# Transposes inside the first half of each tile's products, low halves ahead of the gate logits, and an opening in another order

## The chip, the cores and the metric

One core of a Trainium2 chip runs the whole program. The time is device microseconds of one launch, from the first to the last instruction and what lies around it. The kernel before took 1167.78 us (median of three runs, 1166.98 to 1170.35).

## What is computed

The reference is one macaron layer on `x` of 4 sequences x 512 rows x 512 columns: half a step of a feed-forward block with gated low-rank corrections, latent attention with 32 heads, and the feed-forward block again with the same weights.

```python
x = x + 0.5 * ffn(layernorm(x))
x = x + attn(layernorm(x))        # 32 heads, causal, latent keys of 64, rotary parts of 64
x = x + 0.5 * ffn(layernorm(x))

def ffn(x):
    y = x @ W_base.T + b_base
    z = einsum('bth,erh->bter', x, lora_A[active])          # 4 experts, rank 8
    logits = (x @ router_W.T + router_b)[..., active]
    alpha = softmax(log(domain_prior[active] + EPS) + logits)
    return y + einsum('bteo,bte->bto', einsum('bter,eor->bteo', z, lora_B[active]) * 2.0, alpha)
```

## The kernel before, in words

Every engine has its own program, written out by hand, and runs it strictly in the written order; semaphores are the only ties between them. There is no scheduler: the order of the work is the order of the Python statements, and an instruction that waits holds all that stands behind it on its engine.

The work of a sequence `b` is a row of tiles of 128 rows, and an attention over all its heads. A **feed-forward tile** goes through these steps. ScalarE (in the opening VectorE) normalises the rows, `xn` (`norm`, L1163 and L1275). TensorE transposes them in four pieces into the bank `X[0]` (`transpose_x`, L650). ScalarE rounds the transposed rows to `xT_hi` (`xT_high`, L1037), VectorE takes the rest, `xT_lo` (`xT_low`, L1281). TensorE forms three products (high by high, high by low, low by high) for each of 4 blocks of columns (`ffn_products`, L675), in two halves: half 0 is 12 matmuls of 292 columns (256 outputs, 32 of `z`, 4 gate logits), half 1 is 12 of 256. From the end of half 0, VectorE reads the logits and their maximum (`gate_logits`, L1288 and L1290), ScalarE the exponentials (`gate_exponentials`, L1046), VectorE divides and scales `z` by the gates to `za` (`gate_rows`, L1295, L1297, L1306). TensorE transposes `za` (`transpose_z`, L691), ScalarE and VectorE split it into `zT_hi` (L1042) and `zT_lo` (L1314), and TensorE adds the low-rank correction (`lora`, L700). VectorE adds the tile to the rows (`update_rows`, L1321).

A **down tile** makes the latent queries, keys and values of 128 rows: the same normalising and transposing, then `down_products` (L684), two halves of 6 matmuls of 320 columns, `key_rotary` on VectorE (L1331 to L1334), `down_copies` on ScalarE (L1053 to L1055), `transpose_down` on TensorE (L710), and `ckT_high` and `ckT_low`.

These tiles come in three kinds of stage:

- the **opening** (sequence 0, before its attention): weights are transposed and split first (`transpose_base`, `base_high`, `base_low`, `transpose_lora`, `fill_up` L1358), the statistics of the first rows come in between, `gate_row` is spread to all partitions by a matmul (L800), then 4 feed-forward tiles, which I call F0 to F3 here too, then weight folding and 4 down tiles (these alone keep their order);
- the **mixed stage**, between two attentions, three times (near 319, 592 and 865 us): 12 tiles in the order of the table `ORDER`: the next sequence's first feed-forward tiles F0 to F3, then D0, L0, D1, L1, D2, D3, L2, L3, where D are the next sequence's down tiles and L this sequence's last feed-forward tiles;
- the **last stage** (sequence 3): L0 to L3.

On TensorE, tile i stands as: half 0; the transposes of `za` of tile i-1; the transposes of the rows of tile i+1; if tile i-1 is a down tile, its `transpose_down`; half 1; the correction of tile i-1. On VectorE, tile i stands as: `update_rows` of tile i-2 with its statistics; `gate_logits` of i; `z_low` of i-1; `xT_low` of i+1; `ckT_low`; `gate_rows` of i. On ScalarE: `norm` of i+1, `z_high` of i-1, `xT_high` of i+1, `ckT_high`, `gate_exponentials` of i, `down_copies`.

GpSimd makes the inverse deviations of the rows of down tiles (`down_deviations`, L508 to L531); in the opening it also splits the rotary weights in products of several us (L585, L589). ScalarE's queue has three loads of activation tables in the opening, before L1067, before the logarithm of the prior (L1115) and before a first exponential (L1117).

Of the kernel before, what the change touches and what calls it, by code (L numbers as in the profile page):

```python
# [34 lines left out]
P = 128  # L35
NB, S, D = 4, 512, 512
ST = S // P
KC = D // P
# [69 lines left out]
def build(nc, hidden, w_q_down, w_q_up_nope, w_q_up_rope, w_kv_down, w_k_rope, w_uk, w_uv, w_out,  # L108
          W_base, b_base, lora_A, lora_B, router_W, router_b, domain_prior, active,
          rope_cos, rope_sin, rope_cosT, rope_sinT, out):  # L110
    with ExitStack() as ctx:
# [292 lines left out]
        with nc.Block() as block:  # L404
# [240 lines left out]
            def _(pe):  # L645
# [24 lines left out]
                def ffn_products(b, s, half):  # L670

                    a, z = ((0, W0), (W0, WB))[half]
                    for c in range(KC):
                        for j, (xt, w) in enumerate(((xT_hi, wb_hi), (xT_hi, wb_lo), (xT_lo, wb_hi))):
# [5 lines left out]
                def down_products(b, s, half):  # L680

                    for c in (2 * half, 2 * half + 1):
                        for j, (xt, w) in enumerate(((xT_hi, wd_hi), (xT_hi, wd_lo), (xT_lo, wd_hi))):
# [97 lines left out]

                def opening_queries():
# [11 lines left out]
                def opening():  # L794
# [3 lines left out]
                    pe.wait_ge(turns_one, 1)  # L798
                    pe.wait_ge(gate_in, 16 * 2 * NE)
                    nc.tensor.matmul(gate_ps, cosT[0:1, 0:P], gate_row[:], start=True, stop=True).then_inc(gate_spread, 1)  # L800
                    pe.wait_ge(lora_lo_set, 1)
                    for s in range(FIRST, DOWN):
# [4 lines left out]
                        ffn_products(-1, s, 0)  # L807
                        if s > FIRST:
                            if s == FIRST + 1:
                                pe.wait_ge(up_lo, 1)  # L810
                            transpose_z(-1, s - 1)
                        if s + 1 < DOWN:
                            transpose_x(-1, s + 1)
# [54 lines left out]
                def steps(b, order):  # L868

                    for i, s in enumerate(order):  # L870
                        products = ffn_products if s < DOWN else down_products
                        wait_for_products(b, s)
                        products(b, s, 0)
                        if i and order[i - 1] < DOWN:
                            transpose_z(b, order[i - 1])
                        if i + 1 < len(order):
                            transpose_x(b, order[i + 1])
# [156 lines left out]
            def _(act):  # L1034
# [62 lines left out]
                def opening():  # L1097
# [4 lines left out]
                    for c in range(KC):  # L1102
# [4 lines left out]
                                  .rearrange("q (h d) -> q h d", d=DN)).then_inc(nope_in[0], 16)  # L1107
                    xT_high(-1, FIRST)
# [7 lines left out]
                    act.wait_ge(consts_set, 1)  # L1116
                    nc.scalar.activation(warm_slot[:, 0:1], three_halves[0:1, :], ACT.Exp)  # L1117
# [126 lines left out]
            def _(dve):  # L1244
# [160 lines left out]
                def opening():  # L1405
# [4 lines left out]
                    nc.vector.bn_stats(stats[:, 0, :], x_sb[:, 0, :]).then_inc(stats_set, 1)  # L1410
# [29 lines left out]
                    for s in range(FIRST, DOWN):  # L1440
# [7 lines left out]
                        if s + 1 < DOWN:  # L1448
                            xT_low(-1, s + 1)
# [46 lines left out]
                def mixed_steps(b):  # L1496
                    for i, s in enumerate(ORDER):
# [7 lines left out]
                        if s < DOWN:  # L1505
                            gate_logits(b, s)
# [164 lines left out]
```

## Time and profile before

| | |
|---|---|
| runs | 1170.35, 1166.98, 1167.78 us |
| the profiled execution | 1167.57 us, of which 1165.8 us are the span |
| mean granted TensorE clock | 0.992 of full speed |
| busy share: PE, PEld, DVE, ACT, POOL | 95%, 78%, 78%, 54%, 63% |
| chain that ended last | PE 79%, DVE 7%, POOL 7%, ACT 3% |

PE is TensorE's matmuls, PEld its weight loads, DVE VectorE, ACT ScalarE, POOL GpSimd, SP the engine that issues most transfers. A row of the timeline has the start in us from the span's start, the duration, the engine, the line, the operation, the output and the inputs, and in brackets how long the engine had been idle before and what ended that. A matmul's duration covers its whole way through the array; the distance of starts tells how densely they follow each other.

### The profile page before, as it was taken

The numbers are of one execution on the slowest core, as the hardware profiler recorded it, in microseconds if no ns is written. First come the engines' busy times: TensorE is split into PE (matmuls) and PEld (weight loads), VectorE is DVE, ScalarE is ACT, GpSimd is POOL, SyncE is SP. The second block draws the span as 40 slices with busy tenths as digits, with TensorE's granted clock in tenths as the row PEclk, the third lists the DMA queues.
The fourth block names the chain that finished last, engine by engine and source line by source line (L and its number), as shares of the span: only waits on it lengthen the run. The fifth ranks groups of instructions, "written<-read, shape, count | busy, mean of one in ns | idle before, by whom it ended". The sixth has DMA issues, their size and how long they took to land.

```text
span 1165.8 us, 21866 instructions
## 1 busy us (share of the span) xinstructions
PE 1105.7 (95%) x7284; PEld 906.6 (78%) x7284; DVE 908.2 (78%) x2667; ACT 623.9 (54%) x1733; POOL 740.0 (63%) x951
## 2 busy tenths in 40 slices
PE   5896999999998999999999899999999899999997
PEld 4755788888797788888788678888888678888876
DVE  4767888888676888878776888788867787888855
ACT  3554655555454655555535555655545466555542
POOL 2406977887432978787631887787723598877841
PEclk9998999999999999999999999999999999999998
DMA  9660000000101000000101000000010100000000
GB/s 286 179 194 1 1 1 1 1 1 1 37 10 64 2 1 2 1 1 1 37 1 37 37 2 1 2 1 2 1 37 28 47 1 1 1 1 2 1 1 37
DMA packets 22248, 30.96 MB, mean 27 GB/s; under 512 B 9302, under 2 KB 11094, under 8 KB 21498
## 3 DMA queue, kind: packets, MB, share of 16 engines
q1 hardware_dynamic: 19770, 24.85, 6.7%
q10 hardware_dynamic: 2368, 4.72, 1.2%
q8 instruction: 59, 0.97, 0.3%
q14 instruction: 51, 0.42, 0.1%
HBM read 22.23 MB, written 4.19 MB: 23 GB/s over the span
## 4 chain that ended last, share of the span: by engine, by line
PE 79%; DVE 7%; POOL 7%; ACT 3%; issue 2%; SPq 1%; DMA 1%; POOLq 0%; DVEq 0%
PE Y L983 15%; PE Y L957 12%; PE XZ L942 11%; PE Y L906 10%; PE XZ L922 6%; PE XZ L923 6%; PE XZ L921 5%; PE Y L675 4%; POOL prob L631 3%; PE XZ L675 2%; POOL qT_lo L542 2%; PE XZ L650 2%; POOL q_sums L537 2%; DVE xT_lo L1281 1%; ACT xT_hi L1037 1%
## 5 line engine op out<-in xcount | busy, mean ns | idle before, releaser
L1228 ACT ACTIVATE prob<-XZ,small 128x512 f32<-128x512 f32 (+3 forms) x512 | 266.3, 525 | 282.8 <-DVE small L1622 282.8
L631 POOL TENSOR_TENSOR prob<-prob,small 128x512 f32<-128x512 f32 (+3 forms) x512 | 360.7, 721 | 50.1 <-DVE small L1576 40.4
L1622 DVE CUSTOM_DVE_ANT_0 XZ<-XZ,mask 128x512 f32<-128x512 f32 (+3 forms) x512 | 247.9, 506 | 114.6 <-PE XZ L923 110.5
L537 POOL TENSOR_TENSOR q_sums<-q_sums,q_turned 64x512 f32<-64x512 f32 (+2 forms) x130 | 164.2, 1263 | 201.5 <-DVE q_turned L1564 200.1
L942 PE MATMUL XZ<-ident,prob 128*128 128x128 f32 x1280 | 196.3, 276 | 3.2 <-POOL prob L631 2.9
L921 PE MATMUL XZ<-kT_hi,qT_hi 128*128 128x512 f32 (+3 forms) x512 | 176.9, 345 | 12.7 <-ACT prob L1228 6.8
L542 POOL TENSOR_TENSOR qT_lo<-q_sums,qT_hi 128x512 fp32r<-128x512 f32 (+2 forms) x130 | 165.2, 1271 | 31.9 <-ACT qT_hi L1195 31.8
L942 PEld LDWEIGHTS XZ<-ident,prob 128*128 128x128 f32 x1280 | 149.5, 140 | 43.2 <-POOL prob L631 10.6
L922 PE MATMUL XZ<-kT_lo,qT_hi 128*128 128x512 f32 (+3 forms) x512 | 165.4, 323 | 0.0
L923 PE MATMUL XZ<-kT_hi,qT_lo 128*128 128x512 f32 (+3 forms) x512 | 165.2, 323 | 0.0
L957 PE MATMUL Y<-probT,ckv 128*64 128x384 f32 (+2 forms) x1280 | 152.3, 384 | 0.0
L390 ACT ACTIVATE probT<-XZ 128x512 f32<-128x512 f32 x192 | 114.9, 598 | 66.0 <-PE XZ L942 64.8
L957 PEld LDWEIGHTS Y<-probT,ckv 128*64 128x64 f32 x1280 | 81.8, 136 | 60.7 <-issue 47.3
L921 PEld LDWEIGHTS XZ<-kT_hi,qT_hi 128*128 128x128 f32 x512 | 97.2, 190 | 22.8 <-issue 7.7
L983 PE MATMUL Y<-wo_hi,oT_hi 128*128 128x512 f32 x256 | 110.9, 433 | 1.5 <-DVE x_sb L1580 1.4
L1580 DVE TENSOR_TENSOR x_sb<-Y,x_sb 128x512 f32<-128x512 f32 x128 | 87.8, 686 | 29.4 <-PE Y L983 29.1
L1228 ACT ACTIVATION_READ_ACCUMULATOR prob<-XZ,small 128x1 f32 x512 | 101.9, 199 | 0.0
L923 PEld LDWEIGHTS XZ<-kT_hi,qT_lo 128*128 128x128 f32 x512 | 97.3, 190 | 5.5
L922 PEld LDWEIGHTS XZ<-kT_lo,qT_hi 128*128 128x128 f32 x512 | 97.7, 191 | 4.8
L983 PE MATMUL Y<-wo_hi,oT_lo 128*128 128x512 f32 x256 | 101.1, 395 | 0.0
L983 PE MATMUL Y<-wo_lo,oT_hi 128*128 128x512 f32 x256 | 100.2, 391 | 0.0
L1195 ACT ACTIVATE qT_hi<-q_sums 128x512 fp32r<-128x512 f32 (+2 forms) x130 | 80.2, 617 | 19.0 <-POOL q_sums L537 19.0
(220 smaller groups left out, 2162.0 us busy)
## 6 DMA issues: line engine op xcount, KB each, us to landing
wout_nat<-in_L_attn_w_out_dram SPq DMA_DIRECT2D x16, 512.0 KB, 5.0
out_dram<-x_sb SPq DMA_DIRECT2D x16, 256.0 KB, 2.0
x_next<-_attn_hidden_states_dram SPq DMA_DIRECT2D x12, 256.0 KB, 3.4
x_sb<-x_next SPq DMA_DIRECT2D x12, 256.0 KB, 2.3
wbase_nat<-in_L_ffn_W_base_dram ACTq DMA_DIRECT2D x1, 1024.0 KB, 5.7
x_sb<-_attn_hidden_states_dram ACTq DMA_DIRECT2D x4, 256.0 KB, 7.0
nope_a<-_L_attn_w_q_up_nope_dram ACTq DMA_DIRECT2D x1, 1024.0 KB, 5.4
rope_a<-_L_attn_w_q_up_rope_dram SPq DMA_DIRECT2D x1, 1024.0 KB, 8.0
```

What stands on the lines that cost most here:

```text
L537: nc.gpsimd.tensor_tensor(q, q, turned, ALU.add).then_inc(q_sum_set, 1)
L542: nc.gpsimd.tensor_tensor(qT_lo[par][:, head, cols], q_sums[par][:, head, cols], f32(qT_hi[par][:, head, cols]), ALU.subtract).then_inc(qT ...
L631: last = nc.gpsimd.tensor_tensor(prob[u % RING][:, c:c + w], prob[u % RING][:, c:c + w], inv_sum[:, u % RING, m:m + 1].broadcast_to([P, w] ...
L906: last = nc.tensor.matmul(bank[:, cols], w, c, start=(j == 0), stop=(j == 4))
L921: nc.tensor.matmul(bank[:, c:c + w], high, kT_hi[:, 0:w], start=True, stop=False)
L922: nc.tensor.matmul(bank[:, c:c + w], high, kT_lo[:, 0:w], start=False, stop=False)
L923: last = nc.tensor.matmul(bank[:, c:c + w], low, kT_hi[:, 0:w], start=False, stop=True)
L942: last = nc.tensor.transpose(probT_ps[v % 2][:, at], prob[v % RING][:, at], ident[:])
L957: last = nc.tensor.matmul(o_ps[64 * h:64 * h + 64, column * P:(column + n) * P], ckv[:, j, :], probT[:, HEAD_BLOCKS * h + at:HEAD_BLOCKS * ...
L983: last = nc.tensor.matmul(bank, o[buffer][:, rows], w, start=(k == 0 and j == 0), stop=(k == 1 and j == 2))
L1228: last = nc.scalar.activation(prob[u % RING][:, c:c + w], score_ps[u % 2][:, c:c + w], ACT.Exp, bias=neg_max[:, u % RING, m:m + 1], scale= ...
L1622: last = nc.vector.tensor_tensor_reduce(bank, bank, mask[:, S - w:S], -1.0, HIGHEST, ALU.add, ALU.min, neg_max[:, u % RING, m:m + 1])
```

## The change

The calls stay the same, and so do all operands; one activation is added on ScalarE (a first logarithm). Their order changes in five ways.

1. In `ffn_products` and `down_products` the transposes (`za` of the tile before, rows of the next) are called in the middle of half 0: after 6 of its 12 matmuls, in a down tile after 3 of its 6. `transpose_down` stays behind half 0.
2. On VectorE `z_low` and `xT_low` stand ahead of `gate_logits`.
3. In the opening the spreading of `gate_row` moves from ahead of F0's products into their middle.
4. In the opening VectorE takes the first rows' moments ahead of two weight splits, their deviations, normalising and `fill_up` ahead of the other rows' statistics.
5. ScalarE loads the logarithm's table ahead of the first `xT_high`.

```diff
-                def ffn_products(b, s, half):
+                def ffn_products(b, s, half, inside=None):
                     a, z = ((0, W0), (W0, WB))[half]
                     for c in range(KC):
+                        if c == KC // 2 and inside:
+                            inside()
                         for j, (xt, w) in enumerate(((xT_hi, wb_hi), (xT_hi, wb_lo), (xT_lo, wb_hi))):
...
-                def down_products(b, s, half):
+                def down_products(b, s, half, inside=None):
                     for c in (2 * half, 2 * half + 1):
+                        if c == 1 and inside:
+                            inside()
...
+                def spread_gates():
+                    pe.wait_ge(turns_one, 1)
+                    pe.wait_ge(gate_in, 16 * 2 * NE)
+                    nc.tensor.matmul(gate_ps, cosT[0:1, 0:P], gate_row[:], start=True, stop=True).then_inc(gate_spread, 1)
...
                     transpose_lora()
-                    pe.wait_ge(turns_one, 1)
-                    pe.wait_ge(gate_in, 16 * 2 * NE)
-                    nc.tensor.matmul(gate_ps, cosT[0:1, 0:P], gate_row[:], start=True, stop=True).then_inc(gate_spread, 1)
                     pe.wait_ge(lora_lo_set, 1)
...
-                        ffn_products(-1, s, 0)
-                        if s > FIRST:
-                            if s == FIRST + 1:
-                                pe.wait_ge(up_lo, 1)
-                            transpose_z(-1, s - 1)
-                        if s + 1 < DOWN:
-                            transpose_x(-1, s + 1)
+
+                        def transposes(s=s):
+                            if s == FIRST:
+                                spread_gates()
+                            else:
+                                if s == FIRST + 1:
+                                    pe.wait_ge(up_lo, 1)
+                                transpose_z(-1, s - 1)
+                            if s + 1 < DOWN:
+                                transpose_x(-1, s + 1)
+
+                        ffn_products(-1, s, 0, transposes)
                         ffn_products(-1, s, 1)
...
-                        products(b, s, 0)
-                        if i and order[i - 1] < DOWN:
-                            transpose_z(b, order[i - 1])
-                        if i + 1 < len(order):
-                            transpose_x(b, order[i + 1])
+
+                        def transposes(i=i):
+                            if i and order[i - 1] < DOWN:
+                                transpose_z(b, order[i - 1])
+                            if i + 1 < len(order):
+                                transpose_x(b, order[i + 1])
+
+                        products(b, s, 0, transposes)
                         if i and order[i - 1] >= DOWN:
                             transpose_down(b, order[i - 1])
...
+                    act.wait_ge(consts_set, 1)
+                    nc.scalar.activation(warm_slot[:, 0:1], three_halves[0:1, :], ACT.Ln)
                     xT_high(-1, FIRST)
...
                     nc.scalar.activation(prior_row, prior_raw[:], ACT.Ln).then_inc(prior_ln, 1)
-                    act.wait_ge(consts_set, 1)
-                    nc.scalar.activation(warm_slot[:, 0:1], three_halves[0:1, :], ACT.Exp)
+                    nc.scalar.activation(warm_slot[:, 1:2], three_halves[0:1, :], ACT.Exp)
...
                     nc.vector.bn_stats(stats[:, 0, :], x_sb[:, 0, :]).then_inc(stats_set, 1)
+                    dve.wait_ge(stats_set, 1)
+                    row_moments(FIRST).then_inc(var_set, 1)
                     base_low(2)
                     base_low(3)
-                    dve.wait_ge(stats_set, 1)
-                    row_moments(FIRST).then_inc(var_set, 1)
+                    deviations(0, FIRST, 1, 1)
+                    norm(FIRST)
+                    fill_up()
                     for t in range(1, ST):
                         dve.wait_ge(x_in[t], 16)
                         nc.vector.bn_stats(stats[:, t, :], x_sb[:, t, :]).then_inc(stats_set, 1)
-                    deviations(0, FIRST, 1, 1)
-                    norm(FIRST)
                     dve.wait_ge(stats_set, ST)
...
-                    fill_up()
                     xT_low(-1, FIRST)
...
+                        if i and ORDER[i - 1] < DOWN:
+                            z_low(b, ORDER[i - 1])
+                        if i + 1 < MIXED:
+                            xT_low(b, ORDER[i + 1])
                         if s < DOWN:
                             gate_logits(b, s)
-                        if i and ORDER[i - 1] < DOWN:
-                            z_low(b, ORDER[i - 1])
                         if i == 3:
                             deviations(4 + 2 * b, 0, ST, GROUPS_0 + GROUPS * b + 3)
-                        if i + 1 < MIXED:
-                            xT_low(b, ORDER[i + 1])
```

The opening's loop and `last_steps` move `gate_logits` behind `z_low` and `xT_low` in the same way.

TensorE, mixed stage, tile L0 (the tile after D0): `xn_79` are the rows of D1, `down_91` those of D0, `xT_*_82` and `xT_*_84` L0's transposed rows. Before:

```order
L675 MATMUL Y<-wb_hi,xT_lo_84 128x292
L675 MATMUL Y<-wb_hi,xT_hi_82 128x292
L675 MATMUL Y<-wb_lo,xT_hi_82 128x292
L675 MATMUL Y<-wb_hi,xT_lo_84 128x292
L675 MATMUL Y<-wb_hi,xT_hi_82 128x292
L675 MATMUL Y<-wb_lo,xT_hi_82 128x292
L675 MATMUL Y<-wb_hi,xT_lo_84 128x292
L650 MATMUL XZ<-ident,xn_79 128x128 x4
L710 MATMUL Y<-ident,down_91 128x128 x3
L675 MATMUL Y<-wb_hi,xT_hi_82 128x256
```

And now:

```order
L677 MATMUL Y<-wb_hi,xT_lo_84 128x292
L650 MATMUL XZ<-ident,xn_79 128x128 x4
L677 MATMUL Y<-wb_hi,xT_hi_82 128x292
L677 MATMUL Y<-wb_lo,xT_hi_82 128x292
L677 MATMUL Y<-wb_hi,xT_lo_84 128x292
L677 MATMUL Y<-wb_hi,xT_hi_82 128x292
L677 MATMUL Y<-wb_lo,xT_hi_82 128x292
L677 MATMUL Y<-wb_hi,xT_lo_84 128x292
L714 MATMUL Y<-ident,down_91 128x128 x3
L677 MATMUL Y<-wb_hi,xT_hi_82 128x256
```

The next rows' transposes have moved ahead of six products; the down tile's transposes have not moved.

VectorE, mixed stage, tile F3 (`zT_lo_89` is of F2, `xT_lo_83` of D0, the five `newton` to `shift` rows are the deviations of L0 to L3). Before:

```order
L1288 TENSOR_TENSOR small<-XZ,small 128x4
L1290 TENSOR_REDUCE small<-small 128x1
L1314 TENSOR_TENSOR zT_lo_89<-XZ,zT_hi_87 64x128
L1260 TENSOR_TENSOR newton<-rough 128x4
L1262 TENSOR_TENSOR newton<-newton,var_eps 128x4
L1264 TENSOR_SCALAR newton<-newton 128x4
L1266 TENSOR_TENSOR rstd<-newton,rough 128x4
L1269 SCALAR_TENSOR_TENSOR shift<-moments,rstd 128x4
L1281 TENSOR_TENSOR xT_lo_83<-XZ,xT_hi_81 128x512
L1295 RECIPROCAL small<-small 128x1
L1297 TENSOR_SCALAR small<-small 128x4
L1306 TENSOR_TENSOR za_86<-XZ,small 128x32 x2
```

And now:

```order
L1329 TENSOR_TENSOR zT_lo_89<-XZ,zT_hi_87 64x128
L1296 TENSOR_TENSOR xT_lo_83<-XZ,xT_hi_81 128x512
L1303 TENSOR_TENSOR small<-XZ,small 128x4
L1305 TENSOR_REDUCE small<-small 128x1
L1275 TENSOR_TENSOR newton<-rough 128x4
L1277 TENSOR_TENSOR newton<-newton,var_eps 128x4
L1279 TENSOR_SCALAR newton<-newton 128x4
L1281 TENSOR_TENSOR rstd<-newton,rough 128x4
L1284 SCALAR_TENSOR_TENSOR shift<-moments,rstd 128x4
L1310 RECIPROCAL small<-small 128x1
L1312 TENSOR_SCALAR small<-small 128x4
L1321 TENSOR_TENSOR za_86<-XZ,small 128x32 x2
```

The logits and their maximum (L1288 and L1290, now L1303 and L1305) stand behind `xT_lo`, and the reciprocal, which needs ScalarE's exponentials, follows them with no `xT_lo` in between.

ScalarE, opening, from the first rows' high half to the second's (`xT_hi_81` is F0's, `xT_hi_82` F1's). Before:

```order
L1037 ACTIVATE xT_hi_81<-XZ 128x512
L1110 ACTIVATE wb_hi<-Y 128x4x36
L1113 ACTIVATE lora_up<-XZ 128x512
L1115 ACT_TABLE_LOAD
L1115 ACTIVATE small<-prior_raw 128x4
L1117 ACT_TABLE_LOAD
L1117 ACTIVATE small<-small 1x1
L1037 ACTIVATE xT_hi_82<-XZ 128x512
```

And now:

```order
L1123 ACT_TABLE_LOAD
L1123 ACTIVATE small<-small 1x1
L1051 ACTIVATE xT_hi_81<-XZ 128x512
L1126 ACTIVATE wb_hi<-Y 128x4x36
L1129 ACTIVATE lora_up<-XZ 128x512
L1131 ACTIVATE small<-prior_raw 128x4
L1132 ACT_TABLE_LOAD
L1132 ACTIVATE small<-small 1x1
L1051 ACTIVATE xT_hi_82<-XZ 128x512
```

The logarithm's load has moved to the front; the exponential's load still stands between the prior and F1's high half.

## Rows read from the trace of the kernel before

**Rows 1.** Page, part 1: busy time and share of the span, by engine.

```profile
PE 1105.7 (95%) x7284; PEld 906.6 (78%) x7284; DVE 908.2 (78%) x2667; ACT 623.9 (54%) x1733; POOL 740.0 (63%) x951
```

**Rows 2.** Waits, first mixed stage (317 to 374 us): total us, times, longest.

```profile
PEld Y L675 <- issue: 1.4, 4, 0.5
...
PEld XZ L684 <- issue: 0.5, 1, 0.5
...
PEld Y L684 <- issue: 0.3, 1, 0.3
```

**Rows 3.** Timeline, first mixed stage, tiles F1 and F2: start us, us, engine, line.

```profile
324.62 0.60 PE L650 MATMUL XZ<-ident,xn 128*128 128x128 f32 x4
...
325.75 0.29 ACT L1046 ACTIVATE small<-small 128x4 f32<-128x4 f32 x1
...
325.89 0.69 DVE L1281 TENSOR_TENSOR xT_lo<-XZ,xT_hi 128x512 fp32r<-128x512 f32 x1 [0.47 <-ACT xT_hi L1037]
...
326.03 0.80 ACT L1163 ACTIVATE xn<-x_next,shift,rstd 128x512 f32<-128x512 f32 x1
...
326.50 0.15 DVE L1295 RECIPROCAL small<-small 128x1 f32<-128x1 f32 x1
...
326.95 0.29 DVE L1306 TENSOR_TENSOR za<-Y,small 128x32 f32<-128x32 f32 x2
...
329.88 0.13 DVE L1288 TENSOR_TENSOR small<-Y,small 128x4 f32<-128x4 f32 x1
...
330.24 0.30 ACT L1046 ACTIVATE small<-small 128x4 f32<-128x4 f32 x1 [0.34 <-DVE small L1290]
```

**Rows 4.** Timeline, first mixed stage, tile F3 and the rows of D0.

```profile
329.79 0.18 DVE L1253 BATCH_NORM_AGGREGATE moments<-stats 128x2 f32<-128x6 f32 x1
...
332.55 0.81 ACT L1163 ACTIVATE xn<-x_next,shift,rstd 128x512 f32<-128x512 f32 x1 [1.92 <-POOL shift L531]
...
333.41 0.66 PE L650 MATMUL XZ<-ident,xn 128*128 128x128 f32 x4 [0.31 <-ACT xn L1163]
```

**Rows 5.** Timeline, first mixed stage, tile L0 behind D0, and L0's gates in D1.

```profile
338.90 0.37 PE L675 MATMUL Y<-wb_hi,xT_hi 128*128 128x292 f32 x1
...
339.53 0.83 ACT L1163 ACTIVATE xn<-x_next,shift,rstd 128x512 f32<-128x512 f32 x1
...
340.58 0.60 PE L650 MATMUL XZ<-ident,xn 128*128 128x128 f32 x4
...
343.56 0.29 DVE L1306 TENSOR_TENSOR za<-Y,small 128x32 f32<-128x32 f32 x2
343.91 0.33 PE L691 MATMUL XZ<-ident,za 128*128 128x128 f32 x1
```

**Rows 6.** Timeline, first mixed stage, tile L2 and the first queries behind it.

```profile
359.47 0.66 PE L650 MATMUL XZ<-ident,xn 128*128 128x128 f32 x4 [0.24 <-ACT xn L1163]
...
362.21 0.47 PE L906 MATMUL XZ<-cq_hi,wq_hi 128*128 128x512 f32 x1 [0.34 <-DVE kT_lo L1343]
```

**Rows 7.** Timeline, opening: fill-up, gate spread, table load, F2's exponentials, F3's gates.

```profile
15.89 0.20 DVE L1358 COPY up_nat<-up_b 128x128 f32<-128x128 f32 x1
...
19.52 0.56 PE L800 MATMUL Y<-gate_row,cosT 1*128 1x8 f32 x2 [0.98 <-DMA gate_row<-_L_ffn_domain_prior_dram]
...
20.92 1.28 ACT L1117 ACT_TABLE_LOAD   x1
...
33.90 0.29 ACT L1046 ACTIVATE small<-small 128x4 f32<-128x4 f32 x1
...
39.05 1.72 DVE L1297 TENSOR_SCALAR small<-small 128x4 f32<-128x4 f32 x1
```

**Rows 8.** Timeline, last stage: first product of L0, transposes of L1's rows.

```profile
1142.83 0.58 PE L675 MATMUL XZ<-wb_hi,xT_hi 128*128 128x292 f32 x1 [1.83 <-DVE xT_lo L1281]
...
1145.99 0.72 PEld L650 LDWEIGHTS XZ<-ident,xn 128*128 128x128 f32 x4 [0.26 <-ACT xn L1163]
```

**Rows 9.** Windows, last stage: busy us and counts by engine, granted TensorE clock, DMA share, GB/s.

```profile
1143.00:1148.00 5.00, 5.00 (x22) 4.74 (x23) 1.36 (x8) 1.67 (x5) 1.03 (x2) 0.50 0.01 3
```

More of the change, by code:

```diff
@@ L1444, in opening @@
                             norm(s + 1)
-                        gate_logits(-1, s)
                         if s > FIRST:
@@ L1449, in opening @@
                             xT_low(-1, s + 1)
+                        gate_logits(-1, s)
                         gate_rows(-1, s)
@@ L1544, in last_steps @@
                             update_rows(b, s - 2)
-                        gate_logits(b, s)
                         if s:
@@ L1549, in last_steps @@
                             xT_low(b, s + 1)
+                        gate_logits(b, s)
                         gate_rows(b, s)
```

## The prediction

> **What bounds the kernel now.** I read the engines' shares first, then the waits of one mixed stage, then its timeline tile by tile, then the two ends of the program. TensorE is busy 95% of the span [rows 1], so only its gaps can be won, and any new one counts in full. In the first mixed stage the waits before a tile's first product, which is what low halves ahead of the logits can remove, are 1.4, 0.5 and 0.3 us, 2.2 together [rows 2]. Three such stages give 6.6, the most that edit can bring there. The reader should then look at who feeds the transposes, since the change asks for their inputs sooner and puts six products behind them.
>
> **Two loops, in the old timeline.** From the rows' transposes (324.62) it is 1.27 us to the start of `xT_low` (325.89), which holds VectorE 0.61 (to 326.50); from the logits (329.88) it is 0.36 to the exponentials (330.24); from the exponentials (325.75) 0.28 to the next `norm` (326.03) and 1.20 to `za` (326.95) [rows 3]. From `norm` (332.55) it is 0.86 to the transposes of what it wrote (333.41) [rows 4], and from `za` (343.56) 0.35 to its transposes (343.91) [rows 5]. Twelve products take 1.68 (338.90 to 340.58) [rows 5], so six take 0.84; three down products I take as 0.46, an estimate from 0.84 by columns and count (3 x 320 against 6 x 292).
>
> **The mixed stage with the change.** Moving the transposes makes them wanted 0.84 us sooner in a feed-forward tile. Moving the logits makes the exponentials later: the old ones stood 1.13 behind the rows' transposes (324.62 to 325.75) [rows 3]; the new ones stand 1.27 + 0.61 + 0.36 = 2.24 behind them. From one pair of transposes, the rows after next can then be transposed 2.24 + 0.28 + 0.86 = 3.38 later, and the gates 2.24 + 1.20 + 0.35 = 3.79 later. What TensorE does between: 0.35 for the transposes, 0.87 for the other six products (0.84 and a change of weights), half 1 of 1.47 (0.84 x 2 by 256 to 292 columns), a correction of about 0.47 (an estimate, the length of a 512-column product [rows 6]), and the next six products 0.84: 4.0 in all. Between two feed-forward tiles the loops close (3.38 and 3.79 against 4.0). Around a down tile they don't. Tile by tile, the start of the next tile against its old place (an estimate, good to 0.3 each):
>
> - F0 -0.3: a wait of rows 2 goes. F1 +0.35: no correction stands in F0, so the gates are wanted at 4.0 - 0.47 = 3.53, and come at 3.79; the rest is rounding. F2 +0.1, inside the error.
> - F3 +1.1: D0's rows go through GpSimd; their transposes waited before the change already, 0.31 [rows 4], so all of the 0.84 is lost. The moments that GpSimd starts from (329.79, 2.76 ahead of `norm` [rows 4]) now stand behind VectorE's low half, about 0.5 later (0.61, less what VectorE idled). A removed wait gives 0.3 back.
> - D0 +0.2: F3's gates are wanted behind three down products, 0.35 + 0.87 + 1.47 + 0.47 + 0.46 = 3.6, and come at 3.79.
> - L0 +0.65: `norm` of D1's rows starts at 339.53 and allows 339.53 + 0.86 = 340.39, transposes at 340.58 [rows 5]: a slack of 0.19 against a demand 0.84 sooner. Queued behind the wait: L0's other products and all else of TensorE.
> - D1 -0.05 (gates +0.2, a removed wait -0.3); L1 +0.25 (as L0, plus a removed wait); D2 -0.1; D3 -0.3.
> - L2 +0.8: L3's rows were late before, by 0.24 [rows 6], so the demand 0.84 sooner is lost whole, and six products now stand between these transposes and `transpose_down`, whose copies the first queries waited for (362.21) [rows 6].
>
> The sum is +2.7 a stage, 8.1 for three. The lower bound keeps only waits shown by rows where the slack was gone (L0 0.65, L2 0.84, F3 0.84, together 2.3) and takes off half of the 2.2: +1.2. The upper one leaves the removed waits standing: +3.7. Nothing else hides this: the products put behind the waits were the cover.
>
> **The last stage.** TensorE starts L0 at 1142.83 with idle time before, at a granted clock of 0.50 (the 1.2 GHz level) in 1143 to 1148 [rows 8, 9]: 22 matmuls in 5.00 us. L1's rows are ready only for 1145.99, where TensorE already waited 0.26 [rows 8]. Now six products end at about 1144.4 (1142.83 + 6 x 5.00/22 and the first's start), TensorE idles 1.5, and six products of about 0.23 each, 1.4, come after. L0's later products run faster than that where the clock has risen, and the wait before the next tile's first product goes: I take +0.8, bounds +0.4 and +1.5.
>
> **The opening.** The spread of `gate_row` started at 19.52 behind its DMA [rows 7], so it can't be sooner; behind six products that start when `xT_low` and the split LoRA weights are there it comes between 19.5 and 20.8. `fill_up` stood at 15.89 and did not wait [rows 7]; sooner it may wait for its transfer. From the spread on, the gates, a table load of 1.28 (20.92) and the same two loops lead to the exponentials of F2, at 33.90 before, 14.38 behind the spread [rows 7]. In the new order the low half no longer stands behind logits that wait for the prior; by the loops I get 14.0. F2's exponentials matter since ScalarE's weight copies stand behind them and those feed GpSimd's products, beside which F3's gate division took 1.72 (39.05) [rows 7], not the 0.2 of others. So the opening moves by -0.2, bounds -0.4 (the spread at 19.52) and +0.9 (at 20.8).
>
> **Parts at nothing.** The added logarithm is one column of one row on ScalarE ahead of the first `xT_high`, where ScalarE waits for TensorE; its table load only moves. Without that cover it costs one load, 1.28 [rows 7].
>
> **The sum.** The profiled execution is 1167.57 us, 0.2 under the median of the three runs. 1167.57 + 8.1 + 0.8 - 0.2 = 1176.3. The bounds together give 1167.57 + 3.6 + 0.4 - 0.4 = 1171.2 and 1167.57 + 11.1 + 1.5 + 0.9 = 1181.1.
>
> **The rivals.**
> 1. *Faster: the inputs are in time.* If the rows of the tile after a feed-forward one behind a down tile are ready 0.84 sooner too, only the removed waits remain: -6.6, and -1.0 if the opening's first products start a microsecond sooner, 1160.0. The point that decides is the slack at L0: it must exceed 0.84, and rows 5 show 0.19. For it: between feed-forward tiles the loops close, and `norm` at L0 had no idle time ahead of it [rows 5], so some other order of ScalarE's work could bring it sooner. Against it: three places waited before already [rows 4, 6, 8]. 0.10.
> 2. *Even: stalls and removed waits cancel.* If VectorE's lag doesn't reach the exponentials, only L0, L1 and L2 stall, 0.65 + 0.65 + 0.84 = 2.1 a stage, against 2.2 removed: 1167.57 + 0 + 0.8 = 1168.4, within 1167 to 1171. For it: VectorE was idle 0.3 to 0.5 in each of these tiles [rows 3]. 0.16.
> 3. *The clock.* In the last stage the granted clock was 0.50 while TensorE came out of idle time [rows 9]. If the new gap of 1.5 puts the rise off by as much, the twelve products of half 1 that ran partly at the high level cost up to 12 x 0.23 / 2 = 1.4 more: 1177.7. 0.13.
> 4. *One table load for both functions.* The load at 20.92 follows a logarithm and precedes an exponential [rows 7]. If the logarithm moved ahead made the exponential's load unnecessary, the gates would come up to 1.28 sooner: 1175.0. The order of the changed kernel keeps a load there, and the trace has it after a logarithm. 0.02. The Trainium skill (page "ScalarE: Activation LUTs", section "Table sets: the hidden batching unit") says that one set has both functions, so that a logarithm and then an exponential need one load of about 2.7 us; the trace disagrees on both, with a load between them, of 1.28 us.
>
> **Chances and range.** My forecast, slower by 3.6 to 13.5 us, has 0.59; rivals 3 and 4 are slower too, 0.15: slower by over 0.3% together 0.74 (0.3%, 3.5 us, is about what a measurement of this kernel can tell from no change). Rival 2 has 0.16, and gives "within 0.3%"; rival 1, 0.10, is faster. The range leaves out rival 1 and the lower part of rival 2: 1169 to 1182, the upper end that of the bounds and of the clock. The likeliest cases' own range is 1171.2 to 1181.1.
>
> **What would show it.** Right: in the mixed stages TensorE waits before the transposes of rows (on ScalarE's `norm`) and of gates (on VectorE's `za`), 0.5 to 1.7 us at F3, L0 and L2; the waits before a tile's first product are gone; the first queries stand about 2.7 later from the stage's start; the last stage has a gap of 1.5 behind its sixth product; F2's exponentials in the opening are within 0.5 of 33.90. Wrong: no waits at these transposes behind down tiles (rival 1); or waits, but the exponentials as early behind the rows' transposes as before (rival 2); or a load missing ahead of the first exponential (rival 4).

## The result, and the profile after

The changed kernel took 1176.57 us (median of four runs, 1175.3 to 1177.3) against 1168.07 (four runs of before): the ratio is 1.0069, with a 95% interval of 1.0051 to 1.0087. It is slower by 8.5 us; 1176.3 was predicted. The total is right. The terms it was summed from are not: the two largest were wrong in opposite directions. A table by stage, in us, from starts of TensorE's rows in the two profiled executions (spans 1165.8 and 1174.6; "last row" is the last pair of L700 or L704):

| | before | after | difference | predicted |
|---|---|---|---|---|
| first product of the first mixed stage | 319.12 | 318.53 | -0.6 | -0.2 |
| from there to the last stage's first product | 823.71 | 830.07 | +6.4 | +8.1 |
| from there to TensorE's last row | 19.33 | 21.84 | +2.5 | +0.8 |
| from there to the end of the span | 3.6 | 4.1 | +0.5 | 0 |
| a mixed stage, F0's first product to the first queries | 43.09 | 45.15 | +2.06 | +2.7 |

The busy time of TensorE hardly moved: the page of the changed kernel has 1107.3 us against [rows 1]. What was added is waiting.

```profile
PE 1107.3 (94%) x7284; PEld 906.6 (77%) x7284; DVE 909.0 (77%) x2667; ACT 627.8 (53%) x1734; POOL 740.1 (63%) x951
```

The waits of the changed kernel's first mixed stage (us in total, times, longest), beside [rows 2]. These are waits of PEld, the weight loads:

```profile
PEld XZ L650 <- ACT xn L1178: 4.9, 5, 1.4
PEld XZ L695 <- DVE za L1321: 2.0, 5, 0.6
...
PEld XZ L920 <- issue: 0.2, 1, 0.2
PEld XZ L688 <- issue: 0.2, 1, 0.2
```

The waits before a tile's first product went from 2.2 us to the 0.2 of L688, as the edit promises. In their place stand 4.9 us for normalised rows and 2.0 for scaled gates. Before, these two were 1.7 and 0.4 in the same stage:

```profile
PEld XZ L650 <- ACT xn L1163: 1.7, 3, 0.7
...
PEld XZ L691 <- DVE za L1306: 0.4, 1, 0.4
```

TensorE's timeline says where the rows were late: at F3, L0, L1, D3 and L2. The brackets of these matmul rows are shorter than the waits of the weight loads at the same places (0.95, 0.70, 0.74, 1.13 and 1.42), since a bracket starts at the end of the matmul before, some 0.3 us behind its start.

```profile
332.68 0.66 PE L650 MATMUL XZ<-ident,xn 128*128 128x128 f32 x4 [0.76 <-ACT xn L1178]
...
340.53 0.66 PE L650 MATMUL XZ<-ident,xn 128*128 128x128 f32 x4 [0.47 <-ACT xn L1178]
...
348.30 0.66 PE L650 MATMUL XZ<-ident,xn 128*128 128x128 f32 x4 [0.51 <-ACT xn L1178]
...
356.06 0.66 PE L650 MATMUL XZ<-ident,xn 128*128 128x128 f32 x4 [0.87 <-ACT xn L1178]
...
360.45 0.66 PE L650 MATMUL XZ<-ident,xn 128*128 128x128 f32 x4 [1.18 <-ACT xn L1178]
```

And ScalarE's timeline around L0's wait says what made the rows late. The normalising at L1178 stands behind the three copies of D0 (L1067 to L1069), and the first of them waits 1.14 us for the key rotary on VectorE. The rows end at 340.48, and TensorE's transposes of them start at 340.53. (At F3 it is another engine: there `norm` waited 1.13 us for GpSimd's deviations, L531.)

```profile
339.17 0.33 ACT L1067 ACTIVATE down<-Y 128x192 f32<-128x192 f32 x1 [1.14 <-DVE k_sin L1347]
339.40 0.27 ACT L1068 ACTIVATE down<-Y 128x128 f32<-128x128 f32 x1
339.55 0.23 ACT L1069 ACTIVATE ckv<-Y 128x64 f32<-128x64 f32 x1
339.66 0.82 ACT L1178 ACTIVATE xn<-x_next,shift,rstd 128x512 f32<-128x512 f32 x1
```

In the last stage the gap behind L0's sixth product is there, 1.37 us, and the granted clock stays at half long after it: the products behind the gap start 0.24 to 0.25 us apart. TensorE's timeline (the last row is the first product after the clock's rise), then the windows (busy us and counts of PE, PEld, DVE, ACT, POOL; granted clock; DMA share; GB/s), to be read against [rows 8, 9]:

```profile
1148.60 0.58 PE L677 MATMUL XZ<-wb_hi,xT_hi 128*128 128x292 f32 x1 [1.82 <-DVE xT_lo L1296]
...
1151.77 1.11 PE L650 MATMUL XZ<-ident,xn 128*128 128x128 f32 x4 [1.37 <-ACT xn L1178]
...
1152.92 0.45 PE L677 MATMUL XZ<-wb_lo,xT_hi 128*128 128x292 f32 x1
1153.17 0.45 PE L677 MATMUL XZ<-wb_hi,xT_lo 128*128 128x292 f32 x1
...
1157.87 0.30 PE L677 MATMUL Y<-wb_hi,xT_lo 128*128 128x292 f32 x1
```

```profile
1149.00:1154.00 5.00, 3.63 (x16) 3.28 (x16) 1.27 (x6) 1.41 (x2) 0.86 (x1) 0.50 0.00 0
1154.00:1159.00 5.00, 5.00 (x29) 5.00 (x28) 1.52 (x8) 1.63 (x5) 0.00 (x0) 0.62 0.00 0
```

The opening's rows answer to [rows 7]: the first product starts 1.85 us sooner (18.16 against 20.01), the gate spread 0.66 later, F2's exponentials at 33.44 against 33.90.

```profile
18.16 0.61 PE L677 MATMUL Y<-wb_hi,xT_hi 128*128 128x292 f32 x1 [1.48 <-DVE wb_lo L1442]
...
20.18 0.56 PE L789 MATMUL Y<-gate_row,cosT 1*128 1x8 f32 x2 [0.19 <-DMA gate_row<-_L_ffn_domain_prior_dram]
```

```profile
21.20 1.28 ACT L1132 ACT_TABLE_LOAD   x1
...
33.44 0.30 ACT L1060 ACTIVATE small<-small 128x4 f32<-128x4 f32 x1 [1.02 <-DVE small L1305]
```

### The profile page after: what moved, and what is told of

The parts are those of the page before. It is cut to its first block, busy times and chain, and to the rows that moved or that the text cites. A ratio compares the mean times of both kernels' runs of the same rounds, so it can differ in the third digit from the quotient of the medians.

```text
span 1174.6 us, 21867 instructions
## 1 busy us (share of the span) xinstructions
PE 1107.3 (94%) x7284; PEld 906.6 (77%) x7284; DVE 909.0 (77%) x2667; ACT 627.8 (53%) x1734; POOL 740.1 (63%) x951
## 4 chain that ended last, share of the span: by engine, by line
PE 77%; DVE 8%; POOL 7%; ACT 4%; issue 2%; SPq 1%; DMA 1%; POOLq 0%; DVEq 0%
PE Y L997 15%; PE Y L971 12%; PE XZ L956 11%; PE Y L920 10%; PE XZ L936 6%; PE XZ L937 6%; PE XZ L935 5%; PE Y L677 3%; POOL prob L631 3%; POOL qT_lo L542 2%; PE XZ L650 2%; POOL q_sums L537 2%; PE XZ L677 2%; ACT xn L1178 1%; DVE xT_lo L1296 1%
## 5 line engine op out<-in xcount | busy, mean ns | idle before, releaser
L631 POOL TENSOR_TENSOR prob<-prob,small 128x512 f32<-128x512 f32 (+3 forms) x512 | 360.6, 721 | 50.2 <-DVE small L1591 40.4
```

The source lines that it names most:

```text
L631: last = nc.gpsimd.tensor_tensor(prob[u % RING][:, c:c + w], prob[u % RING][:, c:c + w], inv_sum[:, u % RING, m:m + 1].broadcast_to([P, w] ...
```

## The experiments

Two questions were open: which edit costs what in the mixed stage, and why the last stage lost three times its term. Each kernel is read first by its stage lengths, since these repeat (the three mixed stages of an execution agree within 0.06 us), and only then by its time. The lengths are all from the profiled execution, the column of attention from the first of the three; the time is the median of the kernel's runs (c1's profiled execution took 1162.39):

| kernel | time, us | first mixed stage starts | mixed stage | first queries to the next mixed stage | last stage |
|---|---|---|---|---|---|
| before | 1168.07 | 319.12 | 43.09 | 229.80 | 19.33 |
| changed | 1176.57 | 318.53 | 45.15 | 229.86 | 21.84 |
| a1 mixed stage as before | 1170.32 | 320.54 | 43.10 | 229.77 | 21.61 |
| a2 normalising ahead | 1168.97 | 318.69 | 41.22 | 232.00 | 21.10 |
| a3 last stage, behind half 0 | 1177.44 | 320.16 | 45.11 | 229.75 | 19.74 |
| a4 last stage, gap filled | 1179.08 | 321.70 | 45.15 | 230.84 | 19.71 |
| b1 inside, old VectorE order | 1177.64 | 320.01 | 45.19 | 229.81 | 21.85 |
| b2 behind, new VectorE order | 1181.4 | 321.78 | 45.55 | 229.79 | 21.12 |
| b3 before, normalising ahead | 1164.48 | 319.34 | 42.01 | 230.82 | 19.14 |
| c1 normalising ahead, filled | 1159.97 | 320.53 | 41.21 | 229.79 | 19.26 |
| d1 c1 with two more edits | 1157.13 | 316.94 | 40.62 | 229.75 | 19.26 |
| d2 before, filled | 1166.11 | 319.28 | 43.14 | 229.79 | 18.65 |

The kernels a1 to b3 ran once each, c1 in five runs, d1 in four, d2 in ten.

**a1: the mixed stages in the order of before.**

```diff
-                        products(b, s, 0, transposes)
+                        products(b, s, 0, transposes if alone(b) else None)
+                        if not alone(b):
+                            transposes()
```

and in `mixed_steps` on VectorE `gate_logits` ahead of `z_low` and `xT_low` again.

> The changed kernel with the mixed stages in the order of before (transposes behind half 0, logits ahead of the low halves); opening and last stage as changed. Theory, from the changed trace: a mixed stage costs 2.1 us more (its start moved -0.6, the last stage's first product +5.8, so 6.4 over three), so this gives 1176.4 - 6.4 = 1170.0. Rival, the prediction's own term of 2.7 a stage: 1168.3. A second rival, that the 2.5 to 3 us of the last stage are carried over from the mixed stages: 1167.

It took 1170.32, and the mixed stage went back to 43.10: the mixed stages' loss is the edits in them and nothing carried over. The agreement of the time with 1170.0 is partly luck, for its first mixed stage started 2.0 us later than in the changed kernel, though the program up to there is the same (more on that below). The last stage kept its loss, 21.61.

**a2: the normalising of the tile after next ahead of a down tile's copies.**

```diff
-                        if i + 1 < len(order):
+                        if i + 1 < len(order) and not (i and order[i - 1] >= DOWN):
                             norm(b, order[i + 1])
...
                         if s >= DOWN:
+                            if i + 2 < len(order):
+                                norm(b, order[i + 2])
                             down_copies(b, s)
```

> The changed kernel, with the normalising of the tile after next put ahead of a down tile's three copies on ScalarE. Theory: in L0, L1, D3 and L2 TensorE waits for rows whose normalising stands behind the copies, and those behind the key rotary (0.47 + 0.51 + 0.87 + 1.18 = 3.0 a stage); these four waits go, the waits for gates stay or grow by a few tenths: 2.0 to 3.0 a stage less, 1167.4 to 1170.4. Rival: the lag comes from the logits behind the low halves (the prediction's second loop), so the rows wait for something else soon after and no more than 0.5 a stage comes back: 1175 or more.

The stage fell from 45.15 to 41.22, by 3.9; it is now 1.9 shorter than before the change. The theory's 3.0 was added up from the brackets of matmul rows. By the weight loads the four waits were 0.70, 0.74, 1.13 and 1.42, 4.0 together, and that is what came back. In the waits of its first mixed stage the rows are late once, 0.9 us at F3, and the gates' waits stayed as they were:

```profile
PEld XZ L695 <- DVE za L1323: 2.0, 5, 0.6
...
PEld XZ L650 <- ACT xn L1178: 0.9, 1, 0.9
```

Three stages would give 11.8 us; the time fell by 7.6 only, to 1168.97. That this lies in the theory's range is luck: the stages gained more than forecast, and the next column shows what took it back. The attention behind the first two stages took 2.2 longer, and behind the third 1.2 (there the clock falls once in the changed kernel too). The windows behind the first stage show the granted clock at half twice, some 12 us behind the first queries and again 10 us later, in stretches where the changed kernel has 1.00:

```profile
371.00:373.00 2.00, 1.26 (x4) 1.01 (x4) 1.81 (x3) 0.05 (x1) 0.75 (x1) 0.70 0.52 193
373.00:375.00 2.00, 2.00 (x9) 1.90 (x8) 1.15 (x5) 0.68 (x2) 1.51 (x2) 0.50 0.26 97
...
383.00:385.00 2.00, 2.00 (x8) 1.67 (x7) 1.60 (x3) 0.84 (x3) 2.00 (x4) 0.50 0.03 8
```

**a3: the last stage's first tile with its transposes behind half 0.**

```diff
+                        products(b, s, 0, transposes if not alone(b) or i else None)
+                        if alone(b) and not i:
+                            transposes()
```

> The changed kernel, with the transposes of L1's rows behind half 0 again in the last stage's first tile alone. Theory: the gap of 1.37 us behind six products also puts off the rise of the clock, so the whole 2.5 to 3 us of the last stage come back: 1173.4 to 1173.9. Rival: only the gap itself counts, 0.8 as predicted: 1175.6.

**a4: the same gap filled.** Six matmuls go into a bank that the next half overwrites, ahead of the transposes of L1's rows; the transposes stay where the change put them.

```diff
+                            if alone(b) and i == 0:
+                                for _ in range(6):
+                                    nc.tensor.matmul(XZ[1][:, 1, 0:OH], wb_hi[:, 0, 0:P], wb_hi[:, 0, 0:OH], start=True, stop=True)
                             if i + 1 < len(order):
                                 transpose_x(b, order[i + 1])
```

> The changed kernel, with six matmuls whose results nobody reads put into the gap of the last stage's first tile (they write a bank that the next half overwrites). Theory: the work in the gap lets the granted clock rise as soon as before, so that about 1.3 us come back though the transposes start no sooner: 1175.0, and half 1 of L0 shows 0.12 instead of 0.21 between its later products. Rival: the clock rises by time or by useful work since the stage's start, nothing changes: 1176.4.

As times both missed (1177.44 and 1179.08, not 1174 and 1175): in both the clock fell in the opening, where it had not in the changed kernel's profile, and once more often in the third attention, in a4 also once in the first (230.84). The stage they were made for answers clearly. From its first product to its last it took 19.74 and 19.71 us, 2.1 less than in the changed kernel. In a4 the transposes come 3.17 us after L0's first product, exactly as in the changed kernel (1151.77 - 1148.60), so nothing of the order moved; yet the products right behind them run at full speed, 0.14 apart:

```profile
1153.94 0.58 PE L677 MATMUL XZ<-wb_hi,xT_hi 128*128 128x292 f32 x1 [1.51 <-DVE xT_lo L1299]
...
1155.54 1.48 PE L890 MATMUL XZ<-wb_hi 128*128 128x256 f32 x6
1157.11 1.11 PE L650 MATMUL XZ<-ident,xn 128*128 128x128 f32 x4
...
1158.24 0.30 PE L677 MATMUL XZ<-wb_lo,xT_hi 128*128 128x292 f32 x1
1158.38 0.30 PE L677 MATMUL XZ<-wb_hi,xT_lo 128*128 128x292 f32 x1
```

By the granted clock it rose 9.2 us after L0's first product in the changed kernel and 4.3 after it in a4. In the five kernels with the empty gap it is 7.6 to 9.2, in the four others whose clock is at half at the stage's start (before, a3, a4, b3) 4.3 to 5.4. All five kernels with the empty gap (changed, a1, a2, b1, b2) have a last stage of 21.1 to 21.9; the seven without it have 18.7 to 19.7.

**b1 and b2: one edit of the mixed stage without the other.** b1 has the transposes inside and VectorE's old order (the second edit of a1 alone), b2 the transposes behind half 0 and VectorE's new order (the first edit of a1 alone).

> The changed kernel with VectorE's order of before in the mixed stages alone (logits ahead of the low halves); TensorE's transposes stay inside half 0. Read by the mixed stage's length, first product of F0 to first queries: 43.09 before, 45.15 changed. Theory: transposes sooner are enough for the low halves to be in time, and the waits for gates (2.0 us a stage) mostly go, while the waits for rows behind the copies stay: 43.2 to 43.9. Rival, the prediction's reading that the low halves ahead of the logits are what removes the waits before first products: those come back, 45 or more.

> The changed kernel with the transposes behind half 0 again in the mixed stages alone; VectorE's new order stays (low halves ahead of the logits). Read by the same length (43.09 before, 45.15 changed). Theory: the waits before first products go in part (1.3), and the exponentials come 1.1 later behind the rows' transposes, which is paid behind F0 and in the three down tiles that follow a feed-forward tile (about 0.3 + 3 x 0.6): 43.5 to 44.2. Rival, that the place of the transposes is the whole loss: 41.8, the old length less 1.3.

Both theories missed, and neither rival's reason is what happened, though b1's number is its rival's. b1 has 45.19, no less than the changed kernel, though its waits for gates fell to half:

```profile
PEld XZ L650 <- ACT xn L1178: 5.4, 5, 1.4
...
PEld XZ L695 <- DVE za L1321: 1.0, 3, 0.5
...
PEld Y L688 <- issue: 0.5, 1, 0.5
```

Of the 1.0 that left the gates, some 0.4 turned up at the rows (5.4 against 4.9), all of it at F3, where D0's rows come over GpSimd: the weight loads wait 1.38 there, against 0.95. The other four waits for rows are what they were.

```profile
333.82 0.42 PEld L650 LDWEIGHTS XZ<-ident,xn 128*128 128x128 f32 x4 [1.38 <-ACT xn L1178]
```

Another 0.5 turned up before D0's first product, the one place where a wait before first products came back. So the transposes' place alone removes most of those waits, and VectorE's order, with the transposes inside, is worth nothing in this stage. b2 has 45.55, 2.5 more than before: low halves ahead of the logits cost even more alone than the other edit. Its lost time stands in other places, the gates among them:

```profile
PEld XZ L650 <- ACT xn L1180: 2.0, 3, 0.8
...
PEld XZ L695 <- DVE za L1323: 1.4, 2, 0.8
PEld Y L677 <- issue: 1.1, 3, 0.5
```

The two edits cost 2.1 and 2.5 alone and 2.06 together: they don't add.

**b3: before, with a2's edit.**

> The kernel before, with the normalising of the tile after next put ahead of a down tile's copies. Theory: the waits for rows of 0.41 (D3) and 0.24 (L2) go, so the stage is 0.6 shorter, 42.5, and the time 1.8 less than before where the granted clock doesn't fall elsewhere: 1165.1 to 1166. Rival: these waits had another cause, 43.09.

The stage went from 43.09 to 42.01, by 1.1 and not 0.6, and the kernel took 1164.48 in one run. Here too the theory had counted brackets: the weight loads' waits for rows went from 1.7 to 0.6, 1.1 less. So normalising ahead is worth what it removes of these waits, in both kernels, and a2's 1.9 against before has two parts: 1.1 from the normalising by itself (b3), and 0.8 from the change's edits on top of it (42.01 to 41.22).

```profile
PEld XZ L650 <- ACT xn L1163: 0.6, 1, 0.6
```

**c1: a2 with the gaps filled.** Idle matmuls as in a4, at six places: 12 ahead of the last stage's first transposes, 10 ahead of its first product, 12 in its gap, 6 ahead of a mixed stage's last correction, and 10 and 5 around the first queries of the attention behind it.

```diff
+                def idle_work(bank, n):
+                    for _ in range(n):
+                        nc.tensor.matmul(bank[:, 0:OH], wb_hi[:, 0, 0:P], wb_hi[:, 0, 0:OH], start=True, stop=True)
```

> The kernel with normalising ahead of the copies (stage 41.2, but the granted clock fell to 0.5 twice at the start of each later attention, and the attention took 2.2 longer), plus matmuls whose results nobody reads in TensorE's gaps: in the mixed stages' end, the first gaps of the attention behind them, ahead of the last stage's first product and inside its gap. Theory: the falls of the clock follow the gaps, so the attention returns to 229.8 from the first queries to the next stage and the last stage runs at the high level from its start, 19.3 or less to its last matmul: 1169.0 - 3 x 2.2 - 2 = 1160 to 1163. Rival: the clock falls for another reason (total load), and the added matmuls only cost: 1169 or more.

1159.97, at the theory's lower end, ratio to before 0.9942 (0.9922 to 0.9961). The mixed stage is a2's, 41.21. The attention is back at 229.79, and in the windows of the last stage the clock never falls:

```profile
1132.00:1137.00 5.00, 4.16 (x31) 3.67 (x29) 4.76 (x12) 1.41 (x2) 2.24 (x8) 1.00 0.00 0
1137.00:1142.00 5.00, 3.68 (x28) 3.43 (x28) 1.60 (x9) 1.24 (x2) 1.05 (x2) 1.00 0.00 0
```

**d1: c1 with F3 as before, and the opening's end filled.** For F3 alone the transposes stand behind half 0 and the logits ahead; 22 and 26 idle matmuls stand ahead of the opening's last queries and first scores.

> The filled kernel with two more edits. In F3 alone the transposes stand behind half 0 and the logits ahead of the low half, as before (D0's rows come over GpSimd and cannot be sooner; 0.39 and 0.76 us of waits stood there). And idle matmuls fill TensorE's gaps at the opening's end, ahead of the last down tile's queries and of the first scores, where the granted clock was 0.5 for some 8 us. Theory: the mixed stage from F0 to first queries goes from 41.2 to 40.4 (3 x 0.8), and the clock stays up after the opening (1.5): 1156 to 1157. Rival for F3: the wait moves to the gates of F3 in D0, whose slack was under 0.1, and the stage stays at 41 or more: 1158.5 with the clock's part alone.

1157.13, ratio 0.9897 (0.9865 to 0.9930); it beats both kernels. The stage is 40.62, 0.6 shorter, nearer to the theory's 40.4 than to the rival's 41. The page's row of granted clocks is full from end to end, which no other kernel here shows:

```profile
PE   5898999999999999999999999999999999999997
...
PEclk9999999999999999999999999999999999999999
```

**d2: before, with the fillings of c1 that fit it.**

> The kernel before, with the idle matmuls alone (mixed stages' end, the first gaps of the attention behind it, ahead of the last stage's first product); no order is changed. Theory: the fall of the clock behind the third mixed stage goes (1 us at most) and the last stage's L0 runs at the high level, but L1's rows, ready 3.1 us after L0's start, end its wait as before, so little comes back there: 1165 to 1167. Rival: the clock alone carries the gain of the filled kernel over its twin without: 1161 to 1163.

1166.11, ratio 0.9978 (0.9964 to 0.9992): the filling brings 1.8 us to the old order, and the rival falls. To a2 it brought 9.0, most of it in the three attentions (3 x 2.2). d1 is 9.0 faster than d2. By stages, between the profiled executions, 7.4 are the mixed stages, whose length the filling leaves alone (43.09 and 43.14, 41.22 and 41.21). Another 2.3 are d1's opening, in order and clock together, and its last stage takes 0.6 back (19.26 against 18.65).

## Why the prediction was right, and where it was not

**The sum.** 8.7 us were forecast, 8.8 came between the profiled executions. The mixed stages were put 1.7 too high, the last stage 2.2 too low (with the span's last 0.5), the opening 0.4 too high. An error of 0.1 in the sum is luck; the direction and the rough size were not. The span's last 0.5 is not the change's either: from TensorE's last row to the end it is 3.6 again in a1, a2, a4 and b1, which end with the same instructions, and 4.3 and 4.6 in b2 and a3.

**The mixed stage: right places, size 0.6 too high, one term counted twice.** Lag of each tile's start against before, predicted (running sum of the prediction's terms) and measured:

| | F1 | F2 | F3 | D0 | L0 | D1 | L1 | D2 | D3 | L2 | queries |
|---|---|---|---|---|---|---|---|---|---|---|---|
| predicted | -0.3 | 0.05 | 0.15 | 1.25 | 1.45 | 2.1 | 2.05 | 2.3 | 2.2 | 1.9 | 2.7 |
| measured | -0.26 | -0.17 | -0.32 | 0.66 | 0.71 | 1.41 | 1.22 | 1.57 | 1.48 | 1.44 | 2.06 |

- The steps that rest on a slack read from a row held. L0 was put at +0.65 from the 0.19 of [rows 5] and gave +0.70. F3 was put at +1.1 and gave +0.98. L2 was put at +0.8 from its old wait [rows 6] and gave +0.62.
- The step that failed is "F1 +0.35", with F2's +0.1: the gates were put at 3.79 behind the rows' transposes. In F0 these start at 319.34 and F0's gates are transposed at 322.90, 3.56 later, after a wait of 0.18. The first part of the loop was right: the exponentials stand 2.26 behind the transposes, predicted 2.24. The part too long is the 1.20 from the exponentials to `za`. It was read in the old order, where the low half stood between the two [rows 3]; the new order puts the low half ahead of the logits, where the sum has it a first time. Without it the step takes 0.95. F1 gave +0.09 and F2 -0.15, 0.5 less than the two terms, and that is most of the stage's error of 0.64: every tile behind carried it.

```profile
319.34 0.60 PE L650 MATMUL XZ<-ident,xn 128*128 128x128 f32 x4
...
321.60 0.30 ACT L1060 ACTIVATE small<-small 128x4 f32<-128x4 f32 x1 [1.02 <-DVE small L1305]
...
322.55 0.29 DVE L1321 TENSOR_TENSOR za<-XZ,small 128x32 f32<-128x32 f32 x2
...
322.89 0.14 PEld L695 LDWEIGHTS XZ<-ident,za 128*128 128x128 f32 x1 [0.18 <-DVE za L1321]
```

- What holds the rows of the tile after next was left unnamed. The prediction worked out a loop from the logits over the exponentials to `norm`, and beside it read L0's slack of 0.19 from a row. The loop is there, as the 2.26 shows, but the stage's length does not hang on it: b1 takes it away and the stage stays at 45.19. What holds the rows is named in ScalarE's timeline and shown by a2: `norm` stands behind a down tile's copies, which wait for its key rotary. They did so before the change already. So the slack contained the copies, and L0's size came out right without its cause being known:

```profile
339.05 0.33 ACT L1053 ACTIVATE down<-Y 128x192 f32<-128x192 f32 x1 [1.02 <-DVE k_sin L1332]
```

- D3 was put at -0.3, a removed wait and nothing else; it showed a wait for rows (a bracket of 0.87), and the lag changed by -0.04. The copies again.

**The last stage: the rival was the answer.** The forecast's +0.8 assumed that L0's later products would run faster, the clock having risen by then. Rival 3, the clock's rise put off by the gap, was given 0.13 and 1.4 us. It came true with 2.1 (21.84 against a4's 19.71, where the gap is filled and nothing else moves). The order itself was sized about right: where the clock is full from the stage's start on, the new order takes 0.6 more than the old one (19.26 in c1 and d1, 18.65 in d2). The mistake was to price the gap and the clock apart: the products delayed by the gap are the same that then run at half speed, 0.24 apart instead of 0.14.

**The opening** went as argued in this execution, a little beyond its bound (-0.6 against -0.4). The spread landed within its bounds (20.18, predicted 19.5 to 20.8), `fill_up` waited 0.78 for its transfer, and 1.85 us won at the first product shrank to 0.46 at F2's exponentials and 0.45 at ScalarE's weight copies behind them. But the -0.6 holds only where the clock does not fall in the opening. Where it does, the same opening reaches the mixed stage at 320.0 to 321.8, later than before the change; the prediction has no term for that.

**The other rivals.** Rival 1 fell: the waits stand where its condition said. Rival 2 fell with its condition: VectorE's lag does reach the exponentials (2.26 behind the rows' transposes, 1.13 before). Where the lag is taken away, in b1, the stage is still 2.1 longer than before and not even, for the rows are late at F3 and D3 too, which the rival had left out. Rival 4 fell: the load stays at 21.20, of 1.28 us, between a logarithm and an exponential. On that the Trainium skill (page "ScalarE: Activation LUTs", section "Table sets: the hidden batching unit") says one load for both functions; neither trace agrees, for in both a load of 1.28 us stands between the two.

## What to carry to other kernels

Before asking an engine for an input sooner, find on the producing engine's timeline what the producer stands behind, not only how late it is: here the remedy was to move a normalising past copies that wait for something else. That alone gained 1.1 us a stage, and on top of it the edits that had cost 2.1 gained 0.8. Do not put a wait between products of a stage that starts with idle time without filling it: here the wait put off the clock's rise, and that cost 2.1 us, more than the 1.4 of the wait itself. To add up waits of TensorE, take the weight loads' waits and not the matmul rows' brackets: here two edits gave back 3.9 of 4.0 and 1.1 of 1.1 by the former, while the sums of the brackets were 3.0 and 0.6. Judge an edit of one stage by that stage's length in the trace, for the total hides errors that cancel.

## What was not expected of the hardware

- Where TensorE's clock falls is not fixed by the program. Up to the first mixed stage nine kernels have the changed opening's program (d1 with filling behind it), and that stage started between 316.94 and 321.78. In six of the nine profiles the granted clock was 0.5 for some 3 to 7 us near 42 to 49, in three it was not; in the three with the opening of before it was not either. The stage's start follows it: 318.5 and 318.7 without the fall (316.9 in d1), 320.0 to 320.5 with about 3 us at half, 321.7 and 321.8 with about 7. Whether the new opening makes this fall likelier was not tried.
- With the mixed stages shortened in a2, the clock fell in the attention behind each of the three: 2.2 us (the third against c1). Matmuls whose results nobody reads removed that (c1: 229.79). That the shortening is the cause is not shown: b3 has a fall of 1.0 behind its first stage, but so has a4, whose mixed stages are as long as the changed kernel's.
- Work whose result nobody reads made the program faster: c1 differs from a2 in such matmuls alone and is 9.0 us faster (a2 ran once). d1 issues 7429 matmuls against the changed kernel's 7284 and is 19 us faster, some of it by the order (a2, F3) and some by the clock.
- Not settled: why the output behind TensorE's last row takes 0.5 to 1 us more in some executions, and whether VectorE's old order would help once the normalising stands ahead, where 2.0 us of waits for gates are left.
